# Windowed attention and router on one core: keys ahead of values, halos apart, small router tiles in PSUM, query weights' low half on GpSimd

## The reference

```python
q = _pointwise(Wq, bq, layernorm(x)); k = _pointwise(Wk, bk, ctx); v = _pointwise(Wv, bv, ctx)
# 8 heads of 32 channels, a window of 16 positions around t (8 to the left, 7 to the right, zeros outside)
dots = jnp.einsum('bhdt,bhdtw->bhtw', qh, k_win) * scale
out = jnp.einsum('bhtw,bhdtw->bhdt', jax.nn.softmax(dots, axis=-1), v_win)
x = x + jnp.tanh(g_xattn[0]) * _pointwise(Wo, bo, out)
# router on the rows (b, channel) of layernorm(x), H = 2048
scores = softmax(flat @ router_weight.T + router_bias); topk_w, topk_idx = top_k(scores, 8)
x = x + jnp.tanh(g_ffn[0]) * (flat * topk_w.sum() + w_dense @ expert_bias)
```

## Time and profile before

| | before |
|---|---|
| median of 3 runs (1561.31 to 1566.1) | 1562.54 us |
| the profiled execution, its time | 1564.71 us |
| its span on the core | 1562.6 us |
| mean granted TensorE clock, of full speed | 0.973 |
| busy: PE, DVE, ACT, POOL | 93%, 81%, 73%, 73% |

### The profile page before, as it was taken

One profiled execution on the slowest core, in us unless ns is written; L12 is line 12 of the kernel. 1 busy time (PEld: TensorE's weight loads), 2 busy tenths in 40 slices (PEclk: granted clock), 3 DMA queues, 4 the chain that ended last, 5 costly groups with the idle time before them and its releaser, 6 DMA issues.

```text
span 1562.6 us, 66658 instructions
## 1 busy us (share of the span) xinstructions
PE 1454.7 (93%) x28162; PEld 1190.7 (76%) x28162; DVE 1273.0 (81%) x2970; ACT 1145.1 (73%) x2009; POOL 1147.6 (73%) x1110
## 2 busy tenths in 40 slices
PE   2599999999999999999999999999999999999986
PEld 1477877777888878887887888787878878778764
DVE  4378887889888888988888898888889888788773
ACT  3488777778777877877787787778778787767651
POOL 2487877777787878778787877778777787777661
PEclk9799999999999999999999999999999999999895
DMA  6354455554655455455555645555554555434131
GB/s 202 98 146 122 132 139 133 156 149 101 179 139 138 135 156 153 99 178 137 139 137 153 162 109 163 134 139 137 154 164 111 158 134 139 118 97 132 44 99 67
DMA packets 365576, 210.39 MB, mean 135 GB/s; under 512 B 294496, under 2 KB 295520, under 8 KB 361056
## 3 DMA queue, kind: packets, MB, share of 16 engines
q1 hardware_dynamic: 365280, 206.14, 48.7%
HBM read 136.88 MB, written 33.55 MB: 109 GB/s over the span
## 4 chain that ended last, share of the span: by engine, by line
PE 50%; DVE 33%; issue 8%; POOL 4%; ACT 3%; DMA 1%; SPq 0%; POOLq 0%; ACTq 0%; DVEq 0%
PE ps_j L1099 20%; PE ps_s L1159 8%; PE ps_a L1124 6%; PE ps_r L1201 6%; DVE prob_t L882 5%; PE ps_s L1099 4%; DVE p_sum L872 2%; DVE st_x L889 2%; DVE wq_lo L805 2%; POOL prob L481 2%; PE ps_s L1154 2%; DVE lg L1028 2%; PE ps_a L1178 2%; DVE kv_win L846 2%; DVE neg_max L861 1%
## 5 line engine op out<-in xcount | busy, mean ns | idle before, releaser
L474 POOL TENSOR_TENSOR score<-score,p_inv 128x384 f32<-128x384 f32 x256 | 221.4, 865 | 117.0 <-DVE p_inv L876 113.8
L481 POOL TENSOR_TENSOR prob<-score,prob 128x384 f16<-128x384 f32 x256 | 266.4, 1041 | 35.4 <-ACT prob L633 34.8
L1159 PEld LDWEIGHTS ps_s<-kv_win,q_col 32*32 32x32 f32 x16384 | 194.9, 106 | 55.7 <-issue 55.7
L1159 PE MATMUL ps_s<-kv_win,q_col 32*32 32x48 f32 x16384 | 230.5, 204 | 1.7 <-issue 1.6
L455 POOL TENSOR_TENSOR c_lo<-c_in,c_hi 128x1024 fp32r<-128x1024 f32 x64 | 152.6, 2384 | 99.4 <-ACT c_hi L607 99.4
L882 DVE STREAM_TRANSPOSE prob_t<-prob 128x512 f32<-128x512 f32 x256 | 176.7, 699 | 54.9 <-POOL prob L481 54.7
L1124 PEld LDWEIGHTS ps_a<-prob_t,v_diag 128*128 128x128 f16 x6528 | 174.8, 97 | 51.1 <-DVE prob_t L882 33.4
L1099 PE MATMUL ps_j<-c_hi,wkv_hi 128*128 128x512 f32 x512 | 171.7, 417 | 44.7 <-POOL c_lo L455 30.3
L1124 PE MATMUL ps_a<-prob_t,v_diag 128*128 128x48 f16 (+2 forms) x6528 | 187.2, 183 | 27.3 <-DVE prob_t L882 21.0
L450 POOL TENSOR_TENSOR att_lo<-att,att_hi 128x512 fp32r<-128x512 f32 x128 | 161.5, 1271 | 49.7 <-ACT att_hi L593 48.4
L571 ACT ACTIVATE kv_win<-ps_j,v_bias 128x512 f16<-128x512 f32 x128 | 106.3, 844 | 108.4 <-PE ps_j L1099 108.4
(11 more groups left out here) (149 smaller groups left out, 3333.3 us busy)
## 6 DMA issues: line engine op xcount, KB each, us to landing
v_diag<-v_turn SPq DMA_DIRECT2D x512, 68.0 KB
c_in<-ctx_dram SPq DMA_DIRECT2D x64, 512.0 KB, 4.9
x_in<-x_dram SPq DMA_DIRECT2D x64, 512.0 KB, 5.5
x_res<-x_dram SPq DMA_DIRECT2D x64, 512.0 KB, 4.4
out_dram<-x SPq DMA_DIRECT2D x32, 1024.0 KB, 7.0
c_sq<-ctx_dram SPq DMA_DIRECT2D x60, 512.0 KB, 5.5
x<-ctx_dram SPq DMA_DIRECT2D x4, 512.0 KB, 6.7
x<-experts_dram SPq DMA_DIRECT2D x2, 512.0 KB, 10.4
```

Of the source, the lines that this page charges most:

```text
L474: pool.tensor_tensor(score[:, u], score[:, u], p_inv[:, u, :].unsqueeze(2).to_broadcast([P, HALF, KEYS]), ALU.mult).then_inc(pm_rdy, 1)
L481: pool.tensor_tensor(part(prob[:, u % 2], 1)[:, :, 0:KEYS], score[:, u], part(prob[:, u % 2], 0)[:, :, 0:KEYS], ALU.subtract).then_inc(pl_ ...
L1159: ins = pe.matmul(s[head(h), n * KEYS:(n + 1) * KEYS], q_col[head(h), g, at:at + SUB], kv_win[c % 2][head(h), 0, g, at:at + KEYS], start=F ...
```

## The change

- Each step projects keys ahead of values. The values' copies (`values_high`, `values_low`) move to the next step, and `output` waits for the low half instead of for the keys' copy. `context_high` waits for both projections of the chunk before.
- `halo` is called for keys and for values apart, each with its own semaphores; the dummy instruction at L437 goes.
- wd and lg, the router's small tiles, are regions of the PSUM bank ps_r; a column of wd becomes the SBUF tile wd_end. The router weights' sums come from a DVE reduction and one matmul instead of 32 matmuls.
- The scaled query weights are written to SBUF (wq_ln, in the space of the raw key weights), rounded to wq_hi by ACT, and subtracted by POOL.
- SP issues c_sq, c_in and x_in ahead of the v_diag copies; c_sq is loaded one step later than before in the count of chunks (7 ahead, not 8).
- The opening: c_in is loaded second, chunk 0's keys are projected ahead of the values' scale, x_in is loaded ahead of the query weights, the constants are built after, the gates and the output weights are split in step (-1,3), the experts by ACT and DVE in steps (0,1) to (0,3).
- Semaphores of the softmax are one for each unit u, where each stage had one.

A prime marks work of the chunk before, left over from the step before. The diff, cut to its core (the two lists above stand for its reordered calls):

```diff
+        LOGITS = 0
+        WRSUM = slice(3 * G * E, 3 * G * E + E)
+        wd = ps_r[:, LOGITS:LOGITS + G * E].rearrange("p (g e) -> p g e", g=G)
+        lg = ps_r[:, G * E:2 * G * E].rearrange("p (g e) -> p g e", g=G)
...
-            sp.wait_ge(sq_rdy, NCH + 1)
-            sp.dma_start(c_sq[:], ctx[1, :, cols(1)].rearrange("(g p) t -> p g t", g=G)).then_inc(sq_ld, 16)
...
+                def halo(k, off, right, left, ready):
...
+                            need(pool, ready[g], nth(b, c, off + 1))
...
+                def queries_weight_low():
+
+                    need(pool, wqh_rdy, b + 2)
+                    pool.tensor_tensor(wq_lo[:], wq_ln, wq_hi[:], ALU.subtract).then_inc(wql_rdy, 1)
...
+                    for g in range(G):
+                        act.activation(wq_ln[:, g], wq_raw[:, g], ACT.Copy, scale=rs_in[:, g:g + 1]).then_inc(wqs_rdy, 1)
+                    act.wait_ge(wqs_rdy, (b + 2) * G)
+                    act.activation(wq_hi[:], wq_ln, ACT.Copy).then_inc(wqh_rdy, 1)
...
+                if b == 0 and 1 <= c < 3:
+                    half = slice((c - 1) * (T // 2), c * (T // 2))
+                    act.activation(ex_hi[:, half], ex_staged[:, half], ACT.Copy).then_inc(exh_rdy, 1)
...
+                    dve.tensor_reduce(wr_part[:], wr[:].rearrange("p n e -> p e n"), AX, ALU.add).then_inc(wrp_rdy, 1)
...
+                if live(b, c, 0):
+                    turn(1, 0)
+                if finishing(b, c):
+                    finish(3)
+                if c == 1 and seq(b - 1):
+                    router_weights(b, 0)
+                if c == 0 and seq(b - 1):
+                    ln2(b)
+                if c == 1 and seq(b - 1):
                     router_weights(b, 1)
...
+                    if live(b, c, off + 2):
+                        need(pe, vl_rdy[g], nth(b, c, off + 2))
...
+                if b == -1 and c == 2:
+                    pe.wait_ge(consts, 1)
+                    pe.wait_ge(wkl_rdy, 1)
+                    keys(0, 2)
+                    keys(1, 2)
...
```

More of the change, by code:

```diff
@@ L52 @@
 RSQRT_SEED = 0x5F3759DF
-SCORE_SLOTS = 4
 TOP = 2.0 ** 15
@@ L346, in _ @@
                 sp.dma_start(x1[1][half * E:(half + 1) * E, 0, :], experts).then_inc(r_ld, 16)
-            sp.wait_ge(sq_rdy, NCH + 1)
-            sp.dma_start(c_sq[:], ctx[1, :, cols(1)].rearrange("(g p) t -> p g t", g=G)).then_inc(sq_ld, 16)
             def step(b, c, par):
[L352 to L360, removed]
+                if live(b, c, 7):
+                    ch, db = place(c, 7)
+                    rows_in = ctx[b + db, :, cols(ch)].rearrange("(g p) t -> p g t", g=G)
+                    need(sp, sq_rdy, nth(b, c, 6))
+                    sp.dma_start(c_sq[:], rows_in).then_inc(sq_ld, 16)
                 if live(b, c, 3) and live(b, c, 2):
@@ L411, in _ @@
[L411 to L420, removed]
@@ new lines, in step @@
+                if live(b, c, 1):
+                    x_low(1)
+                if c == 3 and seq(b + 1):
+                    queries_weight_low()
+                if live(b, c, 0):
+                    low(0, 0)
+                    normalise(1, 0)
+                if live(b, c, -1):
+                    residual(0, -1)
+                    residual(1, -1)
+                if live(b, c, 0):
+                    low(1, 0)
+                    normalise(2, 0)
+                if live(b, c, 1) or live(b, c, 2):
+                    halo(0, 1, kr_rdy, kl_rdy, kh_rdy)
@@ L649, in output_bias @@
+                def output_bias(g, off):
+                    ch, _ = place(c, off)
+                    buf = x1[parity(c, off, par)]
+                    need(act, o_mm[g], nth(b, c, off))
                     if ch == 0:
@@ L679, in step @@
                                    ACT.Copy).then_inc(wt_rdy, 1)
-                if before:
-                    attention_high(0)
-                    attention(1)
-                    attention_high(1)
-                if now:
-                    exponent(0)
-                if c == 3 and seq(b + 1) and now:
-                    need(act, ln1_rdy, b + 2)
-                    for g in range(G):
-                        need(act, q_mm[g], nth(b, c, 0))
-                    for g in range(G):
-                        act.activation(wq_hi[:, g], wq_raw[:, g], ACT.Copy, scale=rs_in[:, g:g + 1]).then_inc(wqh_rdy, 1)
@@ L838, in _ @@
-            ROUTER = 15
-            def step(b, c, par):
-                def values_low(g):
-                    rows = kv_win[c % 2][:, 1, g, OWN]
-                    need(dve, vh_rdy[g], nth(b, c, 2))
-                    dve.scalar_tensor_tensor(part(rows, 1), ps_j[g][:], v_bias[parity(c, 2, par)][:, g:g + 1],
+            values_weight_low(0, 0)
+            for ch in range(NCH):
+                dve.wait_ge(x_ld[ch], 16)
+                for g in range(G):
+                    stats_in(g, ch)
@@ L1204, in router, with turn_weights @@
                     ins.then_inc(r_mm, 1)
[L1206 to L1242 removed]
+                def turn_weights():
                     need(pe, wd_rdy, 2 * b)
[L1245 removed]
+                    need(pe, xth_rdy[1], nth(b, c, -2) if live(b, c, -2) else N)
                     for g in range(G):
@@ L1279, in step, with keys @@
-                if before:
-                    rows(0, -1)
-                if live(b, c, 2):
-                    keys(0)
-                    keys(1)
-                if b == -1 and c == 3:
-                    pe.wait_ge(r_ld, 16 * 4)
-                    for k in range(T // P):
-                        ins = pe.matmul(ps_r[:, 0:E], all_ones[:], wr[:, k], start=(k == 0), stop=(k == T // P - 1))
-                    ins.then_inc(sum_mm, 1)
+                def keys(g, off):
+                    need(pe, cl_rdy, nth(b, c, off))
+                    if live(b, c, off - 3):
+                        need(pe, ob_rdy[g], nth(b, c, off - 3))
+                    else:
+                        need(pe, vl_rdy[g], nth(b, c, off - 1))
+                    project(ps_j[g], wkv_hi[:, 0], wkv_lo[:, 0], g, c_hi, c_lo).then_inc(k_mm[g], 1)
@@ new lines, in values, with queries @@
+                def values(g, off):
+                    need(pe, kh_rdy[g], nth(b, c, off))
+                    if c == 2:
+                        need(pe, wvl_rdy, b + 2)
+                    project(ps_j[g], wkv_hi[:, 1], wkv_lo[:, 1], g, c_hi, c_lo).then_inc(v_mm[g], 1)
+                def queries(g, off):
+                    ch, db = place(c, off)
+                    need(pe, xl_rdy, nth(b, c, off))
+                    if ch == 0:
+                        need(pe, wql_rdy, b + db + 1)
+                    need(pe, sh_rdy[2 + g], nth(b, c, off - 1))
+                    project(ps_s[g], wq_hi, wq_lo, g, x_hi, x_lo).then_inc(q_mm[g], 1)
@@ L1291, in _ @@
+                if b == 0 and c == 0:
+                    pe.wait_ge(wrp_rdy, 1)
+                    pe.matmul(ps_r[:, WRSUM], all_ones[:], wr_part[:], start=True, stop=True).then_inc(sum_mm, 1)
             walk(step)
```

1074 lines of the change are left out of this document (538 added, 536 removed).

## The result

The changed kernel took 1639.14 us (1624.79 to 1647.47, 4 runs) against 1564.32 for the kernel before: a ratio of 1.0474, 95% interval 1.0424 to 1.0525. It is 4.7% slower; I had forecast 1545 and at most 1568. The profiled execution took 1647.47 us with a span of 1645.6.

A forecast was written before the change was run, and what follows sets the result against it. TensorE, busy 93% of the span, bounds the kernel. 1562.6 - 21.3 (opening) - 19.5 (kv_win) - 30 (prob_t) + 15 x 2.3 (ln2) + 15 x 0.8 (router) + 15 x 0.3 (mixtures) = 1542.8; after allowances 1545, range 1512 to 1568.

The forecast's parts named there:

- Sum on the profiled span: Whole kernel: gains and stalls added to the earlier span of 1562.6 us give 1542.8, carried to a forecast of 1545.
- the forecast wait for prob_t: At c = 1, TensorE was still to wait for the transposes before an attend, 45 us or more in total.
- SP's order: SP's loads, x_in before v_diag: costed at nothing; without cover, up to 2 us a step.
- The opening: Start of the kernel, up to the second attend of step (0,1): 21.3 us gained, bounds 16 and 24.
- kv_win: TensorE's wait for the values' low half, which frees ps_j for the keys: 19.5 us go, bounds 0 and 19.5.
- ln2 and the router: DVE chains delaying second attends: ln2 stall 2.3 us against 0.46, router 0.8 us, each in 15 sequences.
- the four: Outcomes: the forecast 1545, chance 0.5; no collision 1515, 0.23; slower 1587, 0.12; opening gives back 1558, 0.15.
- Case 3: DVE between turn(1) and turn(3): c_lo and the next POOL instruction catch both chains; 42 us beyond forecast, 1587; chance 0.12.

The follow-up runs named there:

- experiment 3: Changed kernel with both chains moved (w_sum and wd_end in PSUM, ln2 behind the first shift of c = 1): 1637.64 us; with output also cut, 1521.7 us.

## Why the prediction was wrong, by its own steps

**The step that failed** is "Sum on the profiled span": every term was a wait for another engine's result or an instruction's own length, with matmuls at full clock and instructions always at hand. Two terms were missing.
- *Late blocks of instructions.* PE's idle time for "issue" in attends and scores was 51.0 us, 47.3 of it in the 27 holes; the kernel before had 6.5. That is some 41 to 44 us more.
- *Half clock.* From the router's start to the third pair of output matmuls took 7.03 us at half clock (729.62 to 736.65) and 3.94 elsewhere (656.73 to 660.67): 3.1 lost in an episode of 6.8. By that rate the 153.6 us cost some 70, and the 20.5 of the kernel before, which stand in its 1562.6 already, 9: some 61 more. About 14 of the 70 stand behind the forecast wait for prob_t, not behind a late block. PE's busy time, 54 us longer, agrees in size.

Together about 102 to 105 on 1544.8: 1647 to 1650, where 1645.6 was measured. The rate is an estimate from one episode, so that it comes this near is in part luck. That the output's bytes bring the holes is shown by removal: with them gone and nothing else, 1550.84, 6 from the forecast. What share is the clock's is not shown by a run of its own: no run takes the half clock away and leaves the holes. "SP's order", costed at nothing with a bound of 2 us a step for v_diag, looked at who waits for the loaded data and not at what else uses the same DMA engines; and the dense stretch of PE now meets the output, c_sq and c_in. Which of the orders moved, PE's or SP's, brought them together is not separated: undoing SP's alone starves DVE.

**The opening**: right. The second attend of (0,1), c_hi of chunk 1:

```profile
65.14 1.42 PE L1141 MATMUL ps_a<-prob_t,v_diag 128*128 128x32 f16 x51
...
33.08 1.06 ACT L613 ACTIVATE c_hi<-c_in 128x1024 fp32r<-128x1024 f32 x1
```

85.52 - 65.14 = 20.4 gained; forecast 21.3, c_hi near 32.

**kv_win**: right, 0.3 us of PE's wait for it is left.

**ln2 and the router**: right in mechanism and close in size. The timeline of POOL, DVE and PE:

```profile
649.67 2.40 POOL L470 TENSOR_TENSOR c_lo<-c_in,c_hi 128x1024 fp32r<-128x1024 f32 x1 [0.18 <-ACT c_hi L613]
...
649.74 2.35 DVE L787 TENSOR_TENSOR nt_x<-rs_x 128x2 f32<-128x2 f32 x1
...
653.00 1.29 DVE L906 STREAM_TRANSPOSE prob_t<-prob 128x512 f32<-128x512 f32 x2
...
654.39 1.42 PE L1141 MATMUL ps_a<-prob_t,v_diag 128*128 128x32 f16 x51 [1.62 <-DVE prob_t L906]
...
672.67 2.27 DVE L987 CAST wd_cat<-wd_end 128x2 fp32r<-128x2 f32 x1
...
677.05 1.42 PE L1141 MATMUL ps_a<-prob_t,v_diag 128*128 128x32 f16 x51 [1.10 <-DVE prob_t L906]
```

The 128x2 link ends when c_lo does, as in the earlier trace rows; c_hi began 7.8 after the fourth scores (640.77 to 648.54; forecast 7.6). The stalls are 1.62 (forecast 2.3) and 1.10 (0.8), 2.7 a sequence against 3.1. The two lg instructions, now in PSUM, took 0.47 together (0.25 each). But their price was not what the sum said: while blocks are late it is nothing (experiment 3), without them 29 us in 15 sequences.

**Rivals.** None of the four was the cause. Case 3 had the right sign and the wrong place; what the slower side needed was a cause off the chain of data dependencies, namely PE's own instructions coming late. That 1639 lies above case 3's 1587 too shows that the list, and not only its chances, was short. The 1550.84 without the output lies near 1545, but part of that is luck: it has holes of its own (9.4 us of "issue") and 41 us of half clock, against stalls a little smaller than forecast.

## What to carry to other kernels

In this kernel a dense run of small matmuls used up 256 instructions in about 5 us, and the next 256 came over the DMA engines that carry the data. When an order is changed, look where the large transfers fall against that run; idle times of PE put down to "issue" inside a block, at instruction numbers with the same remainder over 256, are the sign. Here moving one 1 MB transfer by a step was worth more than every wait in the sum. And a stall that is taken away gives its time only if nothing behind it was living on it.

## What the hardware showed that I had not expected

- PE's next block of instructions started 4.7 us after its boundary, behind 1.6 MB of data, where about 1 us is usual; PE then stood for 2.5 us though it had no data to wait for. In 27 of 27 holes PE ran on 1.2 to 1.6 us after the packet's end.
- Idle stretches of PE of 1.1 to 2.6 us inside a loop busy for the rest were followed, within 4 us, by 3.4 to 10.2 us at 1.2 GHz, in 18 of the 19 episodes between 80 and 1500 us. The reverse does not hold: of 49 such stretches 31 had no episode behind them; with both chains moved and the output early, 24 of 26 had one. What makes the difference is open. It does not matter what the idle time is for: in the kernel with the output late all ten episodes between 80 and 1425 us followed the 1.6 us wait for prob_t, and with the chains moved as well four were left there.
